# Pair score passes of a graph network: gathered rows stored two chunks at a time behind the additions, index copies of ScalarE one group later

## The reference, cut to what matters

```python
xl = (x @ Wl + bl).reshape(n_nodes, H, C)
xr = (x @ Wr + br).reshape(n_nodes, H, C)
e = jax.nn.leaky_relu(xl[src] + xr[dst], NEG_SLOPE)
alpha = jnp.einsum('ehc,hc->eh', e, att)
m = jax.ops.segment_max(alpha, dst, num_segments=n_nodes)
a = jnp.exp(alpha - m[dst])
denom = jax.ops.segment_sum(a, dst, num_segments=n_nodes)
a = a / (denom[dst] + 1e-16)
out = jax.ops.segment_sum(a[:, :, None] * xl[src], dst, num_segments=n_nodes)
return out.mean(axis=1) + bias
```

## Time and profile before

| | us |
|---|---|
| median of 3 executions | 9958.47 (9952.34 to 9962.12) |
| profiled execution, its own time | 9942.75 |
| span of its instructions | 9940.9 |
| DVE busy in the span | 7246.3 (73%) |
| PE busy in the span | 7218.3 (73%) |
| POOL busy in the span | 5696.2 (57%) |
| first pair score pass, first addition to last score | 3511.3 to 4740.4 |
| second pair score pass, first addition to last score | 5491.3 to 6718.8 |

### The profile page before, as it was taken

How to read it: one execution, slowest core, us unless ns; L and a number is a source line. 1 busy time by engine, 2 the same in 40 slices (tenths; PEclk the granted TensorE clock), 3 DMA queues, 4 the chain that set the end, 5 groups by cost and what they waited for, 6 DMA issues and landing times. The chain is left out here.

```text
span 9940.9 us, 162652 instructions
## 1 busy us (share of the span) xinstructions
PE 7218.3 (73%) x38309; PEld 5091.7 (51%) x38310; DVE 7246.3 (73%) x10360; ACT 2340.0 (24%) x8740; POOL 5696.2 (57%) x5631
## 2 busy tenths in 40 slices
PE   6998998888888656565386566554867875878758
PEld 5776776666666533333375333333754443844437
DVE  8776444777677677777898777778987666876668
ACT  2333555000000111111496111114950000000000
POOL 5776776777677377777000777770007775067750
PEclk9998998999899777777555777775557666976669
DMA  3444554555555377777396777773964443444434
GB/s 102 114 110 111 148 147 116 152 147 147 128 147 147 84 242 248 248 248 243 136 410 265 249 250 248 248 240 143 416 263 107 96 99 68 124 113 98 97 71 120
DMA packets 843231, 1710.71 MB, mean 172 GB/s; under 512 B 385562, under 2 KB 469367, under 8 KB 787609
## 3 DMA queue, kind: packets, MB, share of 16 engines
q1 hardware_dynamic: 456542, 1132.39, 33.0%
q0 software_dynamic: 206896, 411.57, 18.5%
q10 hardware_dynamic: 179712, 165.79, 5.1%
HBM read 1264.25 MB, written 444.85 MB: 172 GB/s over the span
## 5 line engine op out<-in xcount | busy, mean ns | idle before, releaser
L532 POOL DMA_INDIRECT gathered_rows<-node_table,index x2496 | 2375.3, 952 | 928.8 <-issue 750.2
L697 PE MATMUL ps_G<-table_parts,low_onehots 125*128 125x320 bf16 x15600 | 2703.4, 340 | 130.8 <-issue 58.6
L532 POOL DMA_INDIRECT gathered_rows<-xl_table,index x1664 | 1926.9, 1158 | 1415.0 <-PEq L1505 908.7
L552 PE MATMUL ps_sum<-messages,onehots 128*125 128x65 f32 (+3 forms) x13312 | 1968.9, 313 | 494.4 <-DVE messages L1914 185.7
L532 POOL DMA_INDIRECT gathered_rows<-rel_table,index x1456 | 1384.2, 951 | 1555.0 <-ACT index L522 1111.7
L552 PEld LDWEIGHTS ps_sum<-messages,onehots 128*125 128x125 f32 x13312 | 1868.8, 226 | 635.6 <-issue 630.2
L1517 PE MATMUL ps_Z<-xr,onehots_wide 125*128 x3328 | 1475.9, 612 | 981.4 <-DVE z L1565 960.5
L697 PEld LDWEIGHTS ps_G<-table_parts,low_onehots 125*128 125x128 bf16 x15600 | 1676.0, 110 | 992.5 <-issue 74.5
L1517 PEld LDWEIGHTS ps_Z<-xr,onehots_wide 125*128 125x128 f32 x3328 | 841.9, 265 | 1615.3 <-issue 1513.5
L1565 DVE TENSOR_TENSOR z<-gathered_rows,ps_Z 128x650 f32<-128x650 f32 x832 | 653.1, 827 | 647.7 <-DMA gathered_rows<-xl_table,index 647.7
L727 DVE TENSOR_TENSOR rows_by_feature<-ps_G,fifth_onehots 128x320 f32<-128x320 f32 x1040 | 505.6, 486 | 576.8 <-PE ps_G L697 565.7
(11 more groups left out here) (329 smaller groups left out, 6742.9 us busy)
## 6 DMA issues: line engine op xcount, KB each, us to landing
stash_a<-gathered_rows SPq DMA_DIRECT2D x208, 1300.0 KB
kept_rows<-stash_a SPq DMA_DIRECT2D x208, 1300.0 KB, 7.5
onehots<-onehots_kept SPq DMA_DIRECT2D x520, 500.0 KB
onehots_turned<-onehots_turned SPq DMA_DIRECT2D x416, 256.0 KB, 5.3
stash_r<-gathered_rows ACTq DMA_DIRECT2D x208, 272.0 KB
kept_rows<-stash_r SPq DMA_DIRECT2D x208, 272.0 KB, 2.7
low_rows<-low_rows SPq DMA_DIRECT2D x416, 128.0 KB
onehots_kept<-onehots ACTq DMA_DIRECT2D x104, 500.0 KB
```

The lines of the kernel that those rows point to most:

```text
L532: pool.indirect_dma_start(G[:, HALF * k + q, 0:width], None, table, bass.IndirectOffsetOnAxis(IDX[:, k, q:q + 1], 0)).then_inc(gathered[k] ...
L552: return nc.tensor.matmul(ps_sum[0:BN, bass.ds(at, width)], S[:, j, :], M, start=False, stop=True, skip_group_check=True)
L697: last = nc.tensor.matmul(ps_G[:, (fetch * k + g) % 2, 0:D * FIVE], OT[0:BN, k, g, a, :], HP[:, part, a, :, :].rearrange("p f b -> p (f b) ...
```

## The change

SyncE no longer stores a group as a whole when it has landed. It stores two chunks (`PAIRS` = 4 stores of 128 x 650 floats per group), each behind the VectorE addition that reads them, by a wait on `z_made`. The load of the one-hot matrices now stands ahead of the group's stores; its own wait is as before. The counts of `stashed` are four times as high. ScalarE copies the indices of group k a group later: nothing after group 0, index 0 after group 1, index 1 after group 2, and 2 and 3 after group 3. `load_turned`, `gather_loop` and the programs of GpSimd, TensorE and VectorE are the same instructions as before. `stash_group` stays for the relation passes.

```diff
+            PAIRS = HALF // 2
...
                             for k in range(K):
-                                stash_group(sp, G, GW, stash_a, i, k)
-                                if last_turn and k >= K // 2:
-                                    continue
-
-                                ahead, slot = i + (k + K // 2) // K, (k + K // 2) % K
-                                sp.wait_ge(z_made.sem, z_made.at(4 * (K * i + k - 1)))
-                                sp.sem_inc(sp_seen, 1)
-                                load_turned(sp, ST, ahead, slot)
+                                if not (last_turn and k >= K // 2):
+                                    ahead, slot = i + (k + K // 2) // K, (k + K // 2) % K
+                                    sp.wait_ge(z_made.sem, z_made.at(4 * (K * i + k - 1)))
+                                    sp.sem_inc(sp_seen, 1)
+                                    load_turned(sp, ST, ahead, slot)
+                                for e in range(PAIRS):
+                                    j = HALF * k + 2 * e
+                                    sp.wait_ge(z_made.sem, z_made.at(4 * (K * i + k) + e + 1))
+                                    sp.sem_inc(sp_seen, 1)
+                                    sp.dma_start(stash_a[bass.ds(K * i + k, 1), :, 2 * e * GW:2 * (e + 1) * GW].rearrange("o p r -> (o p) r"),
+                                                 G[:, j:j + 2, :].rearrange("p c f -> p (c f)")).then_inc(stashed[k].sem, 16)
...
-                            pool.wait_ge(stashed[k].sem, stashed[k].at(16 * i))
+                            pool.wait_ge(stashed[k].sem, stashed[k].at(16 * PAIRS * i))
...
                                 if m % 4 == 3:
-                                    act.wait_ge(gathered[m // 4].sem, gathered[m // 4].at(16 * HALF * (i + 1)))
-                                    keep_index(act, IDX, src_all, i + 1, m // 4)
+                                    for k in () if m // 4 == 0 else (2, 3) if m // 4 == 3 else (m // 4 - 1,):
+                                        act.wait_ge(gathered[k].sem, gathered[k].at(16 * HALF * (i + 1)))
+                                        keep_index(act, IDX, src_all, i + 1, k)
```

More of the change, by code:

```diff
@@ L1490, in _ @@
                         for k in range(K):
-                            sp.wait_ge(stashed[k].sem, stashed[k].at(16 * TURNS))
+                            sp.wait_ge(stashed[k].sem, stashed[k].at(16 * PAIRS * TURNS))
                     @block.gpsimd
@@ L1601, in _ @@
                         turn(TURNS - 1, True)
-                for c in (*loaded, *stashed):
+                for c in loaded:
                     c.over(16 * TURNS)
+                for c in stashed:
+                    c.over(16 * PAIRS * TURNS)
                 for c in gathered:
```

## The result

| | us |
|---|---|
| changed kernel, median of 4 executions | 9853.83 (9848.27 to 9863.02) |
| kernel before, on the same chip | 9958.97 (9952.34 to 9962.12) |
| ratio | 0.9896, interval 0.9879 to 0.9913 |
| profiled execution, its own time, and its span | 9855.75 and 9853.7 |

The change makes the kernel 1.04% faster, 105 us, where I had forecast no change with 0.58 and this side with 0.29. The time lies 11 us under the range.

A forecast was written before the change was run, and what follows sets the result against it. GpSimd's gathers, some stretched by VectorE's products, were taken as the bound. 200 groups x 0.00 and -1 us for the pass's end, against 9942.75 profiled (15.7 under the median), gave 9957 us, range 9865 to 9990.

The forecast's parts named there:

- the stretches: Some GpSimd gathers take longer than the usual 0.95 us: the fifth of a group 2.14, the eighth 1.55.
- the hold: A gather starting inside VectorE's product (L1572) is held until the product ends, then takes 0.82 us.
- The cover of 24 us: Time between ScalarE's later index copy, about z + 9.4, and GpSimd's need of that index at z + 33.3.
- z: Start of a group's first VectorE addition, the zero point for times within a group.
- what the transfers do to the landing time: Later stores and load end at z + 10.1, gather 8's packets start at z + 10.2; +0.00 to +0.05 us.
- L: Landing time, from the end of a group's eighth gather to the next group's first addition; 2.22 us before.
- a queued gather takes 0.44: Engine time in us summed for each of gathers 6 and 7 between SyncE's transfers, from z + 6.8.
- upper bound of 0.9: Largest growth in us of the landing time, if stores 3 and 4 cost more and gather 8 must wait.
- margin of 0.16: Gather 5 starts only 0.16 us after its product does; a landing longer by more frees it.
- The rival: Faster, the lock slips: longer landing frees gather 5 and shortens the mean period; 9834 to 9904 us, chance 0.28.
- gathers 5 and 8: Fifth and eighth GpSimd gathers of a group, caught inside VectorE's products; while they are, the period is 9.54 + L.
- the rule of held gathers: Gathers starting inside a product end 0.82 us after it, others take 0.95; this sets the group period, 11.76 us before.

The follow-up runs named there:

- x1: Kernel before with only ScalarE's index copies moved a group later, SyncE as before; ratio 1.0001.
- z4: Changed kernel with its four stores issued at the landing, load behind them, for the first six turns of each pass, then the new times; ratio 0.9922.
- z1: Kernel before with two extra 128x256 memsets on VectorE between a group's landing and its first addition; ratio 0.9881.
- z2: Kernel before with two extra memsets and two reduces on VectorE ahead of a group's first addition, about 1.05 us more; ratio 0.9844.
- x4: Changed kernel with the load of one-hot matrices issued when a group's rows have landed, ahead of its first store; ratio 0.9931.
- y4: Kernel before with the product's attention row in PSUM in place of SBUF, and two pair buffers in place of four; ratio 0.9650.
- y2: Kernel before with one extra 128x256 memset on VectorE between a group's landing and its first addition; ratio 0.9999.

## Why the prediction was wrong

**Right.** GpSimd is the bound, the stretches are its loss, and they are made by the product: taking the hold away gives 347 us. The index copies give nothing (x1). The cover of 24 us holds: GpSimd's idle time hasn't grown (1415.0 and 1417.6). ScalarE's waits go as forecast; the waits of 4002 to 4049 after, as in the earlier trace rows, have no line of onehots_wide any more:

```profile
DVE z L1570 <- DMA gathered_rows<-xl_table,index: 12.4, 5, 3.6
...
ACT index L522 <- DMA gathered_rows<-xl_table,index: 3.3, 2, 2.5
```

SyncE issues at z + 1.05 and through 5.45 us, and the load at z + 7.22 (4009.21 - 4001.99), against 6.85 summed. Nothing is gated by a store.

**The step that failed** is the sum behind "what the transfers do to the landing time": 3.34 us of engine time from z + 6.8, engines free at z + 10.1, L + 0.00 to 0.05. The terms of the stores were right (0.88 against 0.85 measured). The two terms "a queued gather takes 0.44" were mis-sized: in z4, with the eighth gather just where the sum had it, 19 packets, fewer than the 32 of one gather (0.166 MB by 5200 bytes), held the engines for 0.653 x 1.6 = 1.04 us, where by the prediction's price they take 19/32 x 0.44 = 0.26. The landing time grew by 0.84 to 0.98, near the upper bound of 0.9 that the prediction had worked out for dearer stores, and far above the margin of 0.16. I took the gathers' price from a stretch in which they ran alone, and used it where SyncE's transfers come in; the dear stretch at 4015.2 of the same trace went unread. Why the packets take so long there stays open.

**The rival came true, in part by luck.** The gathers slip, their mean falls under 1120 ns (1098), and 9853.83 lies in the rival's 9834 to 9904. But that range was worked out for gathers 5 and 8 held by turns with 6 and 1, for an added delay of 0.2 to 0.8, and for L up to 3.1. In the change the delay is 2.4, and at L = 4.58 another pair, 7 and 2, is caught, where there is a gain again. Applied step by step, with one L for all groups, the rule of held gathers gives a period of 11.12 for L = 2.5, 10.99 for 3.3, 11.39 for 3.7 and 11.02 for 4.58. Measured were 11.16 (z1, 2.59), 10.96 (z2, 3.28), 11.41 (x4, 3.71) and 11.25 (the change, 4.58). The last is above the rule because L isn't the same in all groups: most have 11.00, as the rule says, and 35 of 190 have 12.41. That arithmetic needed nothing but the earlier trace rows.

**The chances.** Of the possible L from 2.2 to 5, only two strips give no gain by that rule, one up to about 2.4 and one from about 4.1 to 4.2. A forecast of 0.00 to 0.05 in a strip 0.16 wide, by a sum with terms of 0.9, should not have had 0.58.

**The lock.** The Trainium skill (SBUF — State Buffer, section SBUF: two separate sides) says that VectorE and GpSimd share a port pair as an exclusive lock, which a VectorE instruction with two SBUF inputs takes against a GpSimd one that reads SBUF. y4 agrees: with one input in PSUM no gather is held. The page says that whichever starts first blocks the other; the product that starts 0.03 behind a gather in the earlier trace rows was not delayed, so here only the gather waits.

## What to carry to other kernels

If two engines block each other by the time at which they meet, a delay anywhere in the loop can make the kernel faster. Work out the period for a whole range of the delay before you call a margin safe, and look first for the cause of the block, since taking that away (one operand moved to PSUM) was worth more than three times the change. Price a transfer from several windows, and look for the dearest: the same gather packet took 0.22 us at most in one window of the kernel before and 0.69 in another, and the sum that used the first alone was wrong.

## What the runs showed of the hardware

- A memset of 0.27 us put between a wait and the addition that it guards did not delay the product (y2); two of them, 0.5 us, delayed it by some 0.3 (z1: L 2.59 against 2.20, and 2.82 from addition to product in place of 2.89).
- A gather packet of 5200 bytes takes 0.22 us at most in one window with its queue alone, and 0.69 to 0.88 us on the mean in short stretches, with few or no packets of SyncE about (23.5%, 8.6% and none of the engines' time). The cause was not found.
- A gather that starts 0.03 us or more inside a product with two SBUF operands is held, and ends 0.81 to 0.84 us behind it (all 407 in the changed kernel). No product waited for a gather: in z2, 203 products of the first pass start while a gather runs, without a pause behind VectorE's instruction before, and take 1.48 to 1.49 us.
- A product with one operand in PSUM in place of SBUF is as fast (1.48 us), and never held a gather.
